# Scaling a node table in a two-layer graph network on one core: eight slots for the kept groups, scale columns read in place

## What is computed

```python
def gcn_conv(x, W, b, src, dst, n):
    h = x @ W
    deg = segment_sum(ones, dst, n) + 1.0
    dinv = rsqrt(deg)
    agg = segment_sum(h[src] * (dinv[src] * dinv[dst])[:, None], dst, n)
    return agg + h * (dinv * dinv)[:, None] + b

x = layernorm(x + gcn_conv(relu(gcn_conv(x, W1, b1)), W2, b2))
att = sigmoid(x[src] @ Wa + x[dst] @ Wb + b_att)
aggregated = segment_sum((x[src] @ W_msg + b_msg) * att, dst, n)
h_new = gru(aggregated, x)
x = layernorm(x + batchnorm(h_new))
```

## Time and profile before

| | us |
|---|---|
| median of 3 runs | 1793.31 (1788.44 to 1795.03) |
| the profiled execution | 1792.32 |
| its span in the profile | 1790.5 |

### The profile page before, as it was taken

One profiled execution on the slowest core, in us unless ns is written; L12 is line 12 of the kernel. 1 busy time (PEld: TensorE's weight loads), 2 busy tenths in 40 slices (PEclk: granted clock), 3 DMA queues, 4 the chain that ended last, 5 costly groups with the idle time before them and its releaser, 6 DMA issues.

```text
span 1790.5 us, 35822 instructions
## 1 busy us (share of the span) xinstructions
PE 1516.2 (85%) x8066; PEld 1083.9 (61%) x8066; DVE 1323.1 (74%) x4566; ACT 1258.3 (70%) x3108; POOL 1019.8 (57%) x1010
## 2 busy tenths in 40 slices
PE   6300899999999987999999996999999999986665
PEld 3100687787788766787887873555555555545554
DVE  7818566666666657888888854888888888877787
ACT  6786566666666644777677665777777777767799
POOL 5000776666666627777777746666666666614443
PEclk9755899999999997999999997999999999998898
DMA  8898565543343335998877765777764444429998
GB/s 257 268 332 319 161 193 193 189 168 134 138 140 133 137 128 161 306 303 301 274 251 235 234 214 178 223 235 229 225 192 133 124 127 131 123 86 381 379 322 285
DMA packets 218589, 382.37 MB, mean 214 GB/s; under 512 B 38623, under 2 KB 40892, under 8 KB 218496
## 3 DMA queue, kind: packets, MB, share of 16 engines
q1 hardware_dynamic: 189936, 342.01, 55.2%
q0 software_dynamic: 28560, 39.34, 9.7%
HBM read 222.75 MB, written 177.81 MB: 224 GB/s over the span
## 4 chain that ended last, share of the span: by engine, by line
PE 60%; POOL 13%; DMA 10%; issue 6%; DVE 6%; ACT 4%; SPq 1%; ACTq 0%; DVEq 0%; POOLq 0%
POOL gath L683 13%; PE bank L1359 10%; PE bank L1351 9%; PE bank L1411 5%; PE bank L1413 5%; PE bank L1343 5%; PE bank L1425 5%; PE bank L1415 5%; PE bank L1417 5%; PE bank L1418 5%; DMA page<-YT 3%; DMA gath<-G,ROWI 3%; PE bank L1338 2%; PE bank L1376 2%; ACT page L891 2%
## 5 line engine op out<-in xcount | busy, mean ns | idle before, releaser
L683 POOL DMA_INDIRECT gath<-XP,ROWI x294 | 300.8, 1023 | 302.3 <-DMA XP<-page 146.5
L683 POOL DMA_INDIRECT gath<-MT,ROWI x294 | 325.8, 1108 | 196.0 <-PE bank L1425 111.6
L683 POOL DMA_INDIRECT gath<-G,ROWI x294 | 294.6, 1002 | 119.5 <-issue 83.5
L1359 PEld LDWEIGHTS bank<-w_sb,page 128*128 128x128 f32 x1568 | 190.3, 192 | 46.4 <-issue 46.4
L780 ACT ACTIVATE page<-bank,b_sb 128x512 f32<-128x512 f32 x196 | 124.1, 684 | 113.6 <-PE bank L1351 113.6
L1376 PE MATMUL bank<-gath,onehot 128*128 128x128 f32 x1176 | 164.0, 292 | 44.4 <-DMA gath<-G,ROWI 42.5
L1359 PE MATMUL bank<-w_sb,page 128*128 128x128 f32 x1568 | 190.7, 275 | 0.0
L1091 DVE TENSOR_TENSOR page<-bank,DINV 128x512 f32<-128x512 f32 x98 | 67.8, 691 | 159.0 <-PE bank L1359 159.0
L1351 PE MATMUL bank<-page,w_sb 128*128 128x512 f32 x392 | 184.4, 593 | 0.0
L1376 PEld LDWEIGHTS bank<-gath,onehot 128*128 128x128 f32 x1176 | 147.0, 201 | 48.9 <-issue 34.5
L1445 PE MATMUL bank<-ident,page 128*128 128x128 f32 x784 | 116.1, 297 | 63.1 <-DMA page<-YT 56.7
(11 more groups left out here) (223 smaller groups left out, 3543.2 us busy)
## 6 DMA issues: line engine op xcount, KB each, us to landing
page<-YT SPq DMA_DIRECT2D x196, 256.0 KB, 3.6
MT<-page SPq DMA_DIRECT2D x98, 260.0 KB, 3.2
XP<-page SPq DMA_DIRECT2D x98, 256.0 KB, 2.3
G<-page SPq DMA_DIRECT2D x98, 256.0 KB, 2.0
OWN<-page SPq DMA_DIRECT2D x98, 256.0 KB, 2.2
page<-OWN SPq DMA_DIRECT2D x98, 256.0 KB
YT<-page SPq DMA_DIRECT2D x98, 256.0 KB
page<-AD SPq DMA_DIRECT2D x98, 256.0 KB, 3.8
```

What stands on the lines that cost most here:

```text
L683: nc.gpsimd.indirect_dma_start(gath[k][:, w, 0:width], None, rows, bass.IndirectOffsetOnAxis(ap=ROWI[:, at:at + 1], axis=0), bounds_check= ...
L1359: last = nc.tensor.matmul(bank[6 + k][:, j * D:(j + 1) * D], rows[k][:, j * P:(j + 1) * P], w2_sb[:, h, :], start=(h == 0), stop=(h == 1))
```

## The change

- `scl` and its copies on ScalarE are removed, with the semaphore `s_dd`. Both engines take the scale column from DINV itself, whose address in a loop depends on the group.
- Scaled kept groups use eight slots, `s_all = s_o + s_x`, and `s_st` has eight semaphores; free groups go on with s_x and s_o of four each. Group 44, the first kept one, takes slot 4, which is s_x[0].
- Before the first kept group ScalarE and VectorE wait until all free groups are scaled (`s_done` at FREE), since the pages of s_x come into use. ScalarE no longer waits for `s_half`, and VectorE no longer for `s_dd`.
- The pass has loop bodies of eight groups on SP, ScalarE and VectorE instead of four.
- The waits for all stores are over eight semaphores instead of four.

```diff
-        scl = several("scl", 4, [P, J])
...
+        s_all = s_o + s_x
...
-        x_in, s_st = sems("x_in", 4), sems("s_st", 4)
-        s_dd, s_done, s_half, kept_in = sem("s_dd"), sem("s_done"), sem("s_half"), sem("kept_in")
+        x_in, s_st = sems("x_in", 4), sems("s_st", 8)
+        s_done, s_half, kept_in = sem("s_done"), sem("s_half"), sem("kept_in")
...
+        def scaled_in(g):
+            return s_all[g.slot(8) if g.kept else g.slot(4)]
+        def scaled_st(g):
+            return s_st[g.slot(8) if g.kept else g.slot(4)]
+        def scaled_freed(g):
+            first = FREE + (g.slot(8) - FREE) % 8
+            return g.i * 16 - 16 * (first // 8) + (ROUND if g.slot(8) < 4 else 0) if g.kept else g.dma_freed(4)
+        def wait_scaled_stored(eng):
+            for k in range(8):
+                eng.wait_ge(s_st[k], (ROUND if k < 4 else 0) + 16 * len(range(FREE + (k - FREE) % 8, NG, 8)))
...
                 if g := group_of(3):
-                    k = g.slot(4)
                     done, half = in_register(sp, g.done()), in_register(sp, g.done() - FREE)
                     wait(sp, s_done, done)
                     if g.kept:
                         wait(sp, s_half, half)
-                    sp.dma_start(group_of_table(XP, g), s_o[k]).then_inc(s_st[k], 16)
-            run_pass(sp, scale, 3)
+                    sp.dma_start(group_of_table(XP, g), scaled_in(g)).then_inc(scaled_st(g), 16)
+            run_pass(sp, scale, 3, unroll=8)
...
             def scale(group_of):
                 if g := group_of(0):
-                    k = g.slot(4)
                     if g.fixed and g.index == U - 1:
                         act.wait_ge(run_steps, 1)
                         nc.scalar.activation(win_q[0:NG], win_deg[0:NG], ACT.Sqrt).then_inc(run_steps, 1)
-                    wait(act, s_done, g.freed(4))
-                    if g.kept:
-                        wait(act, s_half, g.freed(4) - FREE)
-                    nc.scalar.activation(scl[k][:], DINV[:, bass.ds(g.index * J, J)], ACT.Copy).then_inc(s_dd, 1)
                     if not g.kept:
-                        wait(act, x_in[k], g.dma(4))
-                    wait(act, s_st[k], g.dma_freed(4))
-                    wait(act, s_dd, g.done())
+                        wait(act, x_in[g.slot(4)], g.dma(4))
+                    elif g.fixed and g.index == FREE:
+                        wait(act, s_done, FREE)
+                    wait(act, scaled_st(g), scaled_freed(g))
                     for j in range(3 if g.kept else 0, J):
                         own = slice(j * D, (j + 1) * D)
-                        last = nc.scalar.activation(s_o[k][:, own], kept(g, j * D, D) if g.kept else s_x[k][:, own],
-                                                    ACT.Copy, scale=scl[k][:, j:j + 1])
+                        last = nc.scalar.activation(scaled_in(g)[:, own], kept(g, j * D, D) if g.kept else s_x[g.slot(4)][:, own],
+                                                    ACT.Copy, scale=DINV[:, bass.ds(g.index * J + j, 1)])
                     last.then_inc(s_done, 1)
-            run_pass(act, scale, 0)
-            wait_all_dmas(act, s_st)
+            run_pass(act, scale, 0, unroll=8)
+            wait_scaled_stored(act)
...
             def scale(group_of):
                 if g := group_of(0):
-                    k = g.slot(4)
-                    wait(dve, s_dd, g.done())
-                    wait(dve, s_st[k], g.dma_freed(4))
+                    if g.fixed and g.index == FREE:
+                        wait(dve, s_done, FREE)
+                    wait(dve, scaled_st(g), scaled_freed(g))
                     for j in range(3):
-                        last = nc.vector.tensor_scalar(s_o[k][:, j * D:(j + 1) * D], kept(g, j * D, D),
-                                                       scl[k][:, j:j + 1], None, ALU.mult)
+                        last = nc.vector.tensor_scalar(scaled_in(g)[:, j * D:(j + 1) * D], kept(g, j * D, D),
+                                                       DINV[:, bass.ds(g.index * J + j, 1)], None, ALU.mult)
                     last.then_inc(s_half, 1)
...
-            run_pass(dve, scale, 0, kept_only=True)
+            run_pass(dve, scale, 0, kept_only=True, unroll=8)
```

More of the change, by code:

```diff
@@ L540, in scale @@
                         wait(sp, s_half, half)
-                    sp.dma_start(group_of_table(XP, g), s_o[k]).then_inc(s_st[k], 16)
-            run_pass(sp, scale, 3)
+                    sp.dma_start(group_of_table(XP, g), scaled_in(g)).then_inc(scaled_st(g), 16)
+            run_pass(sp, scale, 3, unroll=8)
             sp.wait_ge(ready, 1)
-            general_clear(sp, 0, SUM, D, lambda: wait_all_dmas(sp, s_st))
+            general_clear(sp, 0, SUM, D, lambda: wait_scaled_stored(sp))
             def conv(group_of):
@@ L701, in scaled_rows_stored @@
             def scaled_rows_stored():
-                wait_all_dmas(pool, s_st)
+                wait_scaled_stored(pool)
             def conv_rows_stored():
@@ L1061, in _ @@
             general_vector(dve, 0, D, link)
-            wait_all_dmas(dve, s_st)
+            wait_scaled_stored(dve)
             row_b2 = b2_row[:].unsqueeze(1).to_broadcast([P, J, D])
```

## The result

The changed kernel takes 1784.34 us, the median of six runs (1780.58 to 1786.74), where the kernel before takes 1792.96 in six: a ratio of 0.9954 with a 95% interval of 0.9937 to 0.9971. That is 8.6 us less (5.2 to 11.3), just inside the 0.5% that was called no difference here; the forecast was 1787.2. The profiled execution took 1785.98 us.

The account below looks back on a forecast made before the run. The scale stage was taken as near the DMA limit, held by the cycles of its four slots. Profiled 1790.5 less 2.2 less 4.0 plus 0.1 gave 1784.4, own time 1786.2; with 1.0 for the median, 1787.2 us, range 1779 to 1795.

Parts of the forecast that it names:

- Eight slots in the kept part: Kept part of the scale stage: stores' slots no longer bound, 0.795 us a group falls to 0.72, 4.0 us gained.
- upper bound of 6.1: Kept part: the most the eight slots could gain, with VectorE's 0.68 us a group over 53 distances.
- No scl copies and the longer loop: Free part of the scale stage: 1.55 us a group falls to 1.50 over 44 groups, 2.2 us gained.
- the copy was not on the circle: Free part: the copy precedes the wait for x, outside a slot's 5.84 us load-scale-reissue cycle, so 9.7 us was not taken.
- the 13 forecast: Free part, sign of being right: ScalarE waits for x at most groups, some 13 us in all.
- The address work at nothing: Scalings of both engines: working out DINV's column address in the loops costs nothing.
- The waits at the end: End of the scale stage: eight waits for stores instead of four add 0.1 us.
- From 200 us on the same but earlier: Sign of being right: after the scale stage, from 200 us on, everything is the same but earlier.
- The DMA wall as it is: Rival, scale stage: DMA engines already bound it; free part gains 1.5 us at 346 GB/s, kept stays 0.80; 1791.8 us, chance 0.16.
- The full rate: Rival: the whole scale stage reaches the final stage's 384 GB/s, gaining 8.1 and 6.1 us; 1779.2 us, chance 0.14.
- Address work: Rival, kept part: unhidden address work bounds VectorE at 0.985 us a group, 10.1 us lost; 1803.4 us, chance 0.05.
- nothing: Rival, scale stage: each removed wait has another right behind it, so no change; 1793.3 us, chance 0.07.

Follow-up runs that it names:

- e2: The changed kernel with the four scl copies, their semaphore and slots put back, eight slots and loops of eight kept: 1868.33 us, ratio 0.9955 to the kernel before.
- e3: The changed kernel with four slots for all groups, no copies, loops of eight: 1874.04 us, ratio 0.9987 to the kernel before.
- e1: The kernel before with loop bodies of eight groups in the scale pass and nothing else: 1875.97 us, ratio 0.9994.
- e5: The changed kernel with two scalings of a kept group on ScalarE and two on VectorE, not one and three: 1860.11 against 1868.13 us before, ratio 0.9959.
- e4: The changed kernel with fixed DINV columns 0 to 3 for every group, so no column address work in loops: 1868.02 us, ratio 0.9947 to the kernel before.
- e10: The changed kernel unaltered, on the experiments' chips: 1859.94 against 1868.18 us for the kernel before, ratio 0.9957.
- e6: The changed kernel loading only half a tile of x for each free group from the fifth on: 1852.24 us in one execution, free part 60.6 us.
- e8: Scaling in place in eight slots for all groups, meant to store two groups later but with the store's distance left unchanged: 1860.48 us, ratio 0.9964.
- e11: Free groups load x into keep's rows, eight store slots, lag set to 12 but the store's distance behind its load unchanged: 1866.5 us, one execution.
- e12: Free groups load x into keep's rows, lag set to 4 but the store's distance behind its load unchanged: 1861.94 us, one execution.
- in place: The changed kernel with one ring of eight slots for all groups, x loaded, scaled and stored in the same slot: 1860.17 us, ratio 0.9961.

## Why the prediction was right, and where it was not

The time, the direction and the place held: 1784.3 lies in the range, 2.9 us under the forecast. The sum came out well partly because its two large terms missed on opposite sides.

**Eight slots in the kept part: mechanism right, mis-sized.** I took 0.72 us a group and 4.0 us gained; it is 0.68 in the loops and 6.7, over my upper bound of 6.1. The 0.72 was my choice against a bad mesh of three near servers, and no row stood behind it: they mesh without a loss. The bound failed because it priced all 53 distances as in a loop. The 54 stores are issued from 135.45 to 170.70, 0.665 apart in the mean, where before it was 0.796 (136.25 to 178.45): 6.95 us, less 0.29 by which the last store lands later (3.00 against 2.71 after its issue). The first nine, at fixed steps, stand 0.59 apart, and VectorE's first twenty groups 0.60. Two of the three were also priced wrong. For the DMA engines I divided 326 GB/s by a share of 0.87 for 375 GB/s, and they do 387, at a share that passes 1 (387 / 1.02 = 379). By the 358 GB/s of the Trainium skill (DMA: Bandwidth & Descriptors, Specifications) a group could not go below 0.73; this trace disagrees, with the 387. For SP I read 0.58 from two stores issued in 0.91 us, of which the second took 0.33. Those two are at fixed steps, and there the 0.58 is right (0.59 in the changed kernel); in a loop body, where addresses and waits are worked out in registers, they stand 0.65 apart, and 0.28 more at the loop's end. That is far nearer to being the bound than I wrote. VectorE's 0.68 held in the loops by two errors that cancel: most of its boundaries between groups are 0.20 and not 0.26, but the loop's end has a hole of 0.38. Outside them it is no floor. That the slots alone make this gain, e2 and e3 show.

**No scl copies and the longer loop, 2.2 us in the free part: not shown.** The profile after has 1.4 less. But with copies the free part took 68.4, 68.4 and 69.05 us (before, e1, e2) and without them 67.0, 67.4, 68.35, 69.0 and 69.1 (after, e5, e4, e10, e3): means of 68.6 and 68.2, under a spread of 2 us. The ratio of e2, 0.9955, is that of e10, 0.9957. So no run shows the term; any size from nothing to about the forecast fits. That the copy was not on the circle, which kept me from taking 9.7 us, held. ScalarE waits for x 16 times and 9.7 us (the 9.2 of 15 above, and one of 0.5 from 130 us on), not the 13 forecast, as its pitch within the loop is 1.25 to 1.29 and not 1.19; only at the fixed steps does it do twelve scalings in 3.62, 1.2 a group.

**The address work at nothing** held (e4). **The waits at the end**, 0.1, are too small to be seen. **From 200 us on the same but earlier** held within 1.1 us.

**The rivals.** The DMA wall as it is (0.16) would have left the kept part at 0.80: it falls with 387 GB/s. For the free part it is not refuted as a part of the bound: 0.98 busy at 337 GB/s, which is within 3% of the 346 it gave. As the whole of it, e6 speaks against it. The full rate (0.14) falls with the 337 GB/s: it took the final stage's 384 GB/s for what loads and stores one for one can have. That reading had no ground, as the stretches of the final stage in the changed kernel show, where free groups come first and kept groups last:

```profile
1640.00:1660.00 20.00, 12.24 (x80) 9.76 (x80) 13.38 (x75) 15.93 (x46) 7.68 (x10) 0.91 1.06 405
1700.00:1720.00 20.00, 13.99 (x96) 11.88 (x96) 16.86 (x91) 18.14 (x55) 9.12 (x13) 0.91 0.92 311
```

The 405 GB/s are groups with two loads and one store; where it is one load to one store the stage moves 311, with the DMA engines 0.92 busy. The row with which I set the bound was a mean of the two. Nor is the 311 a limit of the DMA engines: ScalarE is busy 18.14 of those 20 us, and 19.79 of the next 20 (to 1740 us, 323 GB/s), so it may be what sets the rate there. No stretch of this case shows how fast one load to one store could go. The transfers of each kind, from 1640 to 1680 and from 1702 to 1740 us, with the median time to landing at the end of the row:

```profile
page<-YT SPq DMA_DIRECT2D x21, 256.0 KB, 5.9
page<-HT SPq DMA_DIRECT2D x20, 256.0 KB, 5.7
out_y<-page SPq DMA_DIRECT2D x20, 256.0 KB, 5.8
...
page<-YT SPq DMA_DIRECT2D x24, 256.0 KB, 3.8
out_y<-page SPq DMA_DIRECT2D x24, 256.0 KB, 3.6
```

The faster stretch has landings of 5.7 to 5.9 us, so it also has more transfers under way. Whether the mix, their number or ScalarE's pace sets the difference stays open; e8, e11 and e12 were to vary the number and did not. Address work (0.05) falls with e4, and "nothing" (0.07) with the result.

No version that computes the whole result beat the changed kernel: two and two (0.9959) and in place (0.9961) stand at its ratio on these chips (0.9957).

## What to carry to other kernels

Where an engine stops behind a store's landing although the DMA engines have room, give the stores more slots, and price the next bound from each server at its steady pace: its issue queue back to back with the register work and waits of a step, and once around the loop, not from one pair of issues. A copy that shortens an engine's step is worth nothing while that engine waits for a load. A parameter named lag may set only a range: look at the new trace's issue order before the run is read as a test.

## What I had not expected of the hardware

- A full DMA share says little on the rate. At shares of 0.92 to 1.06 the same 256 KB transfers ran at 311 GB/s (one load to one store, final stage, with ScalarE nearly always busy), 337 (the same, scale stage), 387 (stores alone) and 405 (two loads to one store). The last two pass the 358 GB/s per core named above. The Trainium skill (HBM Reference, Specifications (TRN2)) says that a core streaming alone measures about 425, well above its share; the trace agrees in that 387 and 405 lie between the two.
- SP issues a store every 0.65 us in a loop, of which the issue itself is 0.33, and needs 0.93 across the loop's end; at fixed steps it is 0.59. At the loop's pace 256 KB stores make 383 GB/s against the 385 to 387 that the DMA engines move, so one queue is only just enough for them.
- VectorE stands still for 0.38 us at the end of its loop of eight steps (in four of the turns), 0.21 when the column is fixed (e4): part of the address work sits there, once in eight groups.
